# Stages 1 and 2 of a four-stage transformer block in a new order: batch 0 normalised on chip, six matmuls of constants ahead of the first weight

## The chip, the cores and the metric

The kernel runs on one core of a Trainium2 chip. The metric is the device time in microseconds (us) of one execution; lower is better. The five engines run side by side and are kept in step by semaphores: TensorE (PE, weight loads shown as PEld), VectorE (DVE), ScalarE (ACT), GpSimd (POOL) and SyncE (SP), which here only issues DMAs.

## What is computed

Input `x` is 4 batches of 512 tokens and 512 features in float32. Four residual stages follow one another, each on the layer-normalised stream:

```python
x = x + gelu(einsum('bds,st->bdt', ln(x), einsum('ds,td->st', w1, w2) * sparse_mask) + b2)   # stage 1
x = x + ffn(ln(x), ffn_weight, ffn_bias, centroids, assignments)                             # stage 2
x = x + attention(ln(x), Wqkv, bqkv, Wo, bo)                                                 # stage 3
x = x + ffn(ln(x), ffn_weight, ffn_bias, centroids, assignments)                             # stage 4

def ffn(x, weight, bias, centroids, assignments):
    hits = softmax(x @ centroids.T / 0.1) > 0.01
    rows = any(hits, axis=0)[assignments]          # one mask of output rows, over ALL tokens
    return where(any(hits, axis=1)[:, None] & rows[None, :], x @ weight.T + bias, 0)
```

The row mask of stages 2 and 4 needs the cluster hits of all 2048 tokens, so stage 3 can't begin before the last token of stage 2 has its logits.

## The kernel before

**Tiling.** A tile is 128 tokens by 512 features; there are 16, `n = 4 b + t` for batch `b` (`NB` = 4) and tile `t` (`TPB` = 4). `KC` = 4 is the number of 128-wide chunks of a feature axis. A float32 product is made of three fast matmuls on operands split in a rounded high part (`_hi`, written by ScalarE) and the rest (`_lo`, by VectorE or GpSimd): a_hi w_hi + a_lo w_hi + a_hi w_lo. The helper `products` (L991 to L999) issues these, so nearly all matmuls carry line L997; one tile of a 512 x 512 product is 12 matmuls of 128x512. PSUM has four banks for transposes (`t_bank`) and four for products (`m_bank`), used in turn.

**One list of steps.** `schedule()` (L31) writes one list of steps (kind, what, batch, tile). Each engine's program walks the same list and issues what it has in each step, so the list is the order of every engine's queue, and an engine that waits in a step holds all its later steps. The steps that matter here:
- `w2`, `w1` c: ScalarE and VectorE split a chunk of the two stage-1 weights. `M attn` c: TensorE multiplies it, 12 matmuls (L1070 to L1076 for the first chunk, L997 behind).
- `mask_attn` (L857, VectorE): times the sparse mask. `colmean` (L1091, TensorE): column means by a matmul with a constant. `center_attn` (L871, VectorE), `split_attn` (L739 ScalarE, L861 VectorE): subtract the means, split. The centred weight stands in for the mean of the layer norm, so `y1` can be made from raw `x` and scaled by `rstd` afterwards.
- `split_x` (L721 ScalarE, L647 GpSimd): splits `x` transposed, which comes from memory transposed (`xt`). `M y1`: 12 matmuls a tile. `scaled` (L892 VectorE) scales and adds b2, then Gelu (L735 ScalarE); `x1` (L898 VectorE) adds it to the stream.
- `stats` (L845, L846 VectorE; L635, L636 GpSimd, for stage 3 also `nbias` L639): variance and `rstd` = variance to the power -0.5, per tile. `norm` (L694 ScalarE): the normalised tile, for stage 3.
- `center_f`, `center_c` (L882 VectorE, L652 and L656 GpSimd, L725 and L730 ScalarE): centre the stage-2 weight and the centroids. `T` (L1060 TensorE): four transposes to a t_bank; its `hi` is L715 (ScalarE) and its `lo` L832 (VectorE), step `lo`.
- `M cl2` (L1125): cluster logits of a batch, 8 matmuls; `T tc2`, `logit2`, `prob2`: their softmax (L801 ScalarE, L953 to L974 VectorE). `M dn2`: the dense product of a tile; ScalarE evacuates it (L759), GpSimd adds the bias (L663). `best2`, `mask2` (L1164, L1171): the row mask. `early`: a part of a product issued ahead of the rest.

**Order.** In stages 1 and 2 a loop over batches 1 to 3 does, for each tile, `T x2` of the batch before, `M y1`, `lo x2`, the residual with its stats, `scaled`; then `M cl2` of the batch before; then four `M dn2` of it, beside stats and `split_x` of the next batch.

**DMA queue.** SP issues in this order: eight chunks of w2 and w1 (256 KB each), `ffn` (1 MB), `cen`, `sparse` (1 MB), `x` of batch 0 (1 MB), `xt` of batch 0 in two halves (1 MB), b2, `x` of batch 1. Then it waits for the last `T ffn` and issues `xt` 1 and more.

## Time and profile before

| | us |
|---|---|
| three runs | 330.07, 329.35, 327.91 |
| median | 329.35 |
| profiled execution, whole | 328.85 |
| its span, first to last instruction | 327.0 |

All rows come from the one profiled execution; times in them are us from the start of its span unless marked ns. A row of the waits names the engine and line that waited, what released it, and the total, the count and the longest. A row of the stretches gives the busy time of each engine with its count of instructions, then PEclk, TensorE's granted clock as a share of 2.4 GHz, whose low level, 1.2 GHz, is 0.5. Matmuls are pipelined: their busy times overlap, and the distance from start to start is what one costs. Mean granted clock over the span: 0.950.

### The profile page before, as it was taken

To read this page: it belongs to the slowest core of one execution; us is meant where nothing else is said; L and a number is where in the kernel's file an instruction comes from. 1 tells how busy PE (TensorE), PEld (TensorE's weight loads), DVE (VectorE), ACT (ScalarE), POOL (GpSimd) and SP (SyncE) were. 2 spreads that over 40 slices of the span, in tenths; PEclk is the share of its full clock that TensorE was granted. 3 is DMA by queue.
4 is the path that set the end of the run, shared out by engine and by line. 5 is a ranking of instruction groups with operands and counts; after the bars stand their busy time and mean duration, and the time that the engine had idled before them with its cause. 6 is when DMAs were issued, how large, how long until landed. Compare 5 with 4: busy or idle time off the path is not lost.

```text
span 327.0 us, 4206 instructions
## 1 busy us (share of the span) xinstructions
PE 282.6 (86%) x1356; PEld 228.5 (70%) x1356; DVE 243.7 (75%) x450; ACT 146.8 (45%) x266; POOL 166.2 (51%) x246
## 2 busy tenths in 40 slices
PE   3966939899969979977999899999997999988790
PEld 3835828688858868756988687878785787867670
DVE  3697588684777467867279769789787897689796
ACT  5463432275237423637266346752537526514300
POOL 1046059379747913318934379174952665117221
PEclk9995978999979997999899999999999999999976
DMA  7990488300000000000000000000000000000066
GB/s 234 355 357 1 157 293 299 121 3 0 0 2 0 1 0 2 0 0 2 0 1 0 3 0 3 0 0 2 0 1 1 2 0 0 2 0 0 2 256 258
DMA packets 11013, 19.27 MB, mean 59 GB/s; under 512 B 1072, under 2 KB 2608, under 8 KB 10992
## 3 DMA queue, kind: packets, MB, share of 16 engines
q1 hardware_dynamic: 10992, 19.01, 16.8%
q8 instruction: 11, 0.18, 0.2%
q14 instruction: 10, 0.08, 0.1%
HBM read 14.81 MB, written 4.19 MB: 58 GB/s over the span
## 4 chain that ended last, share of the span: by engine, by line
PE 43%; DVE 30%; issue 9%; ACT 8%; POOL 5%; DMA 3%; SPq 1%; DVEq 0%; ACTq 0%
PE m_bank L997 34%; DVE st L845 5%; PE t_bank L1060 4%; PE m_bank L1125 4%; DMA xt_other<-in_L_ffn_weight 3%; DVE x_tok L898 3%; DVE y_tok L892 2%; ACT even_hi L715 2%; DVE even_lo L832 2%; DVE x_tok L912 2%; DVE w2t_lo L832 2%; DVE y_tok L904 2%; DVE x_tok L917 2%; POOL rstd L636 2%; DVE mx L936 2%
## 5 line engine op out<-in xcount | busy, mean ns | idle before, releaser
L635 POOL TENSOR_SCALAR ve<-mv 128x1 f32<-128x1 f32 x64 | 16.6, 259 | 99.5 <-DVE mv L846 99.1
L663 POOL TENSOR_TENSOR y_tok<-y_tok,bias_f 128x512 f32<-128x512 f32 x32 | 42.3, 1335 | 30.0 <-ACT y_tok L759 30.0
L845 DVE BATCH_NORM_STATS2 st<-x_tok 128x6 f32<-128x512 f32 x64 | 44.2, 691 | 1.7
L759 ACT ACTIVATE y_tok<-m_bank,rstd 128x512 f32<-128x512 f32 x32 | 21.9, 684 | 44.5 <-PE m_bank L997 44.4
L636 POOL TENSOR_TENSOR rstd<-ve,half 128x1 f32<-128x1 f32 x64 | 37.1, 580 | 5.3
L997 PE MATMUL m_bank<-ffn_hi,even_hi 128*128 128x512 f32 x96 | 39.2, 409 | 0.0
L997 PE MATMUL m_bank<-ffn_lo,even_hi 128*128 128x512 f32 x96 | 37.6, 392 | 0.0
L997 PE MATMUL m_bank<-ffn_hi,even_lo 128*128 128x512 f32 x96 | 37.5, 390 | 0.0
L997 PE MATMUL m_bank<-attn_hi,odd_hi 128*128 128x512 f32 x64 | 28.3, 442 | 10.1 <-POOL odd_lo L647 10.1
L832 DVE TENSOR_TENSOR even_lo<-t_bank,even_hi 128x512 fp32r<-128x512 f32 x24 | 16.2, 685 | 22.9 <-ACT even_hi L715 22.9
L735 ACT ACTIVATE y_tok<-y_tok 128x512 f32<-128x512 f32 x16 | 10.0, 630 | 42.1 <-DVE y_tok L892 42.1
L997 PE MATMUL m_bank<-attn_lo,odd_hi 128*128 128x512 f32 x64 | 26.5, 415 | 0.0
L997 PE MATMUL m_bank<-attn_hi,odd_lo 128*128 128x512 f32 x64 | 26.5, 413 | 0.0
L997 PE MATMUL m_bank<-odd_hi,wqkv_hi 128*128 128x512 f32 (+1 forms) x60 | 22.5, 375 | 0.7 <-DVE odd_lo L832 0.6
L832 DVE TENSOR_TENSOR odd_lo<-t_bank,odd_hi 128x512 fp32r<-128x512 f32 x24 | 15.8, 681 | 9.6 <-ACT odd_hi L715 9.5
L997 PEld LDWEIGHTS m_bank<-attn_hi,odd_hi 128*128 128x128 f32 x64 | 13.1, 205 | 13.0 <-DVE y_tok L892 5.7
L997 PE MATMUL m_bank<-odd_lo,wqkv_hi 128*128 128x512 f32 (+1 forms) x60 | 21.6, 361 | 0.0
L997 PE MATMUL m_bank<-odd_hi,wqkv_lo 128*128 128x512 f32 (+1 forms) x60 | 21.6, 360 | 0.0
L997 PEld LDWEIGHTS m_bank<-ffn_lo,even_hi 128*128 128x128 f32 x96 | 18.1, 188 | 4.0
L674 POOL TENSOR_TENSOR x_tok<-x_tok,bo 128x512 f32<-128x512 f32 x16 | 20.7, 1298 | 0.0
L997 PEld LDWEIGHTS m_bank<-ffn_hi,even_lo 128*128 128x128 f32 x96 | 18.2, 190 | 3.3
L997 PEld LDWEIGHTS m_bank<-ffn_hi,even_hi 128*128 128x128 f32 x96 | 18.2, 190 | 3.2
(142 smaller groups left out, 717.5 us busy)
## 6 DMA issues: line engine op xcount, KB each, us to landing
x_tok<-in_L_attn_a_x SPq DMA_DIRECT2D x4, 1024.0 KB, 10.9
out<-x_tok SPq DMA_DIRECT2D x16, 256.0 KB, 2.2
xt_other<-in_L_attn_a_xt SPq DMA_DIRECT2D x2, 1024.0 KB, 5.2
w_raw<-in_L_attn_a_w SPq DMA_DIRECT2D x4, 256.0 KB, 4.5
y_tok<-in_L_attn_a_w SPq DMA_DIRECT2D x4, 256.0 KB, 4.9
xt_other<-in_L_ffn_weight SPq DMA_DIRECT2D x1, 1024.0 KB, 8.7
y_tok<-in_L_attn_a_sparse_mask SPq DMA_DIRECT2D x1, 1024.0 KB, 10.4
xn_odd<-in_L_attn_a_xt SPq DMA_DIRECT2D x2, 512.0 KB, 13.4
```

The costliest lines, as they stand in the source:

```text
L635: link(pool.tensor_scalar(ve[:, i:i + 1], mv[:, i, 1:2], EPS, None, ALU.add))
L636: ins = pool.tensor_tensor(rstd[:, i:i + 1], ve[:, i:i + 1], half[:, :], ALU.pow)
L663: pool.tensor_tensor(y_tok[:, n, :], y_tok[:, n, :], bias_f[:, :], ALU.add).then_inc(biased, 1)
L674: pool.tensor_tensor(x_tok[:, n, :], x_tok[:, n, :], bo[:, :], ALU.add).then_inc(bo_added, 1)
L735: act.activation(gelu[:, n % 2, :], gelu[:, n % 2, :], ACT.Gelu).then_inc(gelu_done, 1)
L759: act.activation(y_tok[:, n, :], bank[:, :], ACT.Identity, scale=rstd[:, i:i + 1]).then_inc(m_act, 1)
L832: dve.tensor_tensor(lo, bank_view(what, t_bank[j % T_BANKS]), f32(hi), ALU.subtract).then_inc(t_free, 1)
L845: link(dve.bn_stats(st[:, at % 2, :], x_tok[:, n, :]))
L898: dve.tensor_tensor(x_tok[:, n, :], x_tok[:, n, :], gelu[:, n % 2, :], ALU.add).then_inc(x1_done, 1)
L997: ins = pe.matmul(bank, a, w, start=(first and n == 0), stop=(last and n == count - 1))
L1060: ins = pe.transpose(bank[:, c * r:(c + 1) * r], blk, ident[0:r, 0:r])
L1125: ins = pe.matmul(bank[:, tokens], cen_hl[:, c, :], a[:, c, tokens], start=(c + h == 0), stop=(c == KC - 1 and h == 1))
```

## The change

- Batch 0 of stage 1 is normalised on chip: `stats`, `rstd` and `norm` of its tiles, transposes `T x1` of the normalised tiles and their split take the place of `xt` of batch 0. Its `y1` is multiplied by the uncentred weight (`split_raw`, new), with no scale behind it. The centred weight is made later and used by batches 1 to 3. `split_attn`'s low part moves from VectorE to GpSimd.
- `rstd` becomes a step of its own: one tile at a time for stage 1 batch 0 and for stage 3; otherwise (stage 1 of batches 1 to 3, stages 2 and 4) one instruction for the four tiles of a batch.
- In the loop over batches, `T x2` of a batch moves beside `M dn2` of the one before, `M cl2` goes behind a `y1` or `dn2` tile, and stats of stage 2 move behind `scaled`. In the tail, `cl2` of the last batch is issued in two halves and a third `dn2` tile comes ahead of the mask.
- SP's queue: `x` of batch 0 comes in two halves right behind the weights, then `sparse`, b2, `ffn`, `x` 1; `xt` of batch 0 is gone; `cen` comes behind a wait for the last `T x1`.
- TensorE issues `WARM` = 6 matmuls of constants (identity by a constant matrix, 128 columns each) before its first step.

The diff, cut to its core (lines removed from `schedule()` are left out, the order before is told above):

```diff
@@ -23,6 +23,7 @@
 SCALE = float(DH) ** -0.5
 T_BANKS = 4
 M_BANKS = 4
+WARM = 6
 FREED_BY_VECTOR = ("attn", "y1", "q", "k", "pv", "wo")
@@ -63,94 +64,133 @@
         step(what, "", b, t)
         step("stats", stage, b, t)
+        if stage == 3 or t == TPB - 1:
+            step("rstd", stage, b, t)
     for c in range(KC):
         step("w2", "", 0, c)
         step("w1", "", 0, c)
+        if c == KC - 1:
+            for t in range(TPB):
+                step("stats", 1, 0, t)
+                step("rstd", 1, 0, t)
+                step("norm", 1, 0, t)
+            step("T", "x1", 0, 0)
+            step("T", "x1", 0, 1)
         step("M", "attn", 0, c)
+    step("lo", "x1", 0, 0)
+    step("lo", "x1", 0, 1)
+    step("T", "x1", 0, 2)
+    step("T", "x1", 0, 3)
+    step("mask_attn", "", 0, 0)
+    step("mask_attn", "", 0, 1)
+    step("split_raw", "", 0, 0)
+    step("mask_attn", "", 0, 2)
+    step("split_raw", "", 0, 1)
+    step("mask_attn", "", 0, 3)
+    step("split_raw", "", 0, 2)
+    step("split_raw", "", 0, 3)
+    step("lo", "x1", 0, 2)
+    step("lo", "x1", 0, 3)
+    step("M", "y1", 0, 0)
+    step("M", "y1", 0, 1)
     for c in range(KC):
         step("center_f", "", 0, c)
...
     step("colmean", "", 0, 0)
...
+    step("scaled", "", 0, 0)
+    step("scaled", "", 0, 1)
+    step("M", "y1", 0, 2)
     step("center_attn", "", 0, 0)
     for t in range(1, TPB):
         step("center_attn", "", 0, t)
         step("split_attn", "", 0, t - 1)
     step("split_attn", "", 0, TPB - 1)
...
+    step("x1", "", 0, 0)
+    step("T", "ffn", 0, 0)
+    step("M", "y1", 0, 3)
+    step("scaled", "", 0, 2)
+    step("split_x", "", 1, 0)
+    step("split_x", "", 1, 1)
     step("lo", "ffn", 0, 0)
...
+    step("x1", "", 0, 1)
+    step("T", "ffn", 0, 1)
     step("T", "ffn", 0, 2)
     step("T", "ffn", 0, 3)
...
+    step("scaled", "", 0, 3)
+    step("lo", "ffn", 0, 1)
+    step("x1", "", 0, 2)
     step("lo", "ffn", 0, 2)
...
     step("lo", "ffn", 0, 3)
...
+    step("x1", "", 0, 3)
+    step("split_x", "", 1, 2)
+    step("split_x", "", 1, 3)
+    step("center_c", "", 0, 0)
+    for t in range(TPB):
+        step("stats", 1, 1, t)
+    step("rstd", 1, 1, TPB - 1)
     step("T", "cen", 0, 0)
...
     for b in range(1, NB):
         for t in range(TPB):
...
+            if b == 1:
+                step("T", "x2", 0, t)
             step("M", "y1", b, t)
...
+            if b == 1:
+                if t == 0:
+                    step("lo", "cen", 0, 0)
+                step("lo", "x2", 0, t)
+            if t:
+                step("x1", "", b, t - 1)
+                if b == NB - 1:
+                    step("stats", 2, b, t - 1)
             step("scaled", "", b, t)
...
+            if b == 1:
+                step("stats", 2, 0, t)
+            elif t == 0:
+                step("M", "cl2", b - 1, 0)
+            elif t == 1:
+                step("T", "tc2", b - 1, 0)
+                step("logit2", "", b - 1, 0)
+            elif t == 2:
+                step("prob2", "", b - 1, 0)
+        if b == 1:
+            step("rstd", 2, 0, TPB - 1)
+            step("onehot", "", 0, 0)
+        if b == NB - 1:
+            break
+        for t in range(TPB):
+            step("M", "dn2", b - 1, t)
+            if b == 1 and t == 0:
+                step("M", "cl2", 0, 0)
+            if t == 0:
+                step("x1", "", b, TPB - 1)
+            if b == 1 and t == 1:
+                step("T", "tc2", 0, 0)
+                step("logit2", "", 0, 0)
+            step("T", "x2", b, t)
+            step("lo", "x2", b, t)
+            step("stats", 2, b, t)
+            step("split_x", "", b + 1, t)
+            step("stats", 1, b + 1, t)
+            if b == 1 and t == 2:
+                step("prob2", "", 0, 0)
+        step("rstd", 2, b, TPB - 1)
+        step("rstd", 1, b + 1, TPB - 1)
     b = NB - 1
     step("T", "x2", b, 0)
     step("T", "x2", b, 1)
+    step("x1", "", b, TPB - 1)
     step("lo", "x2", b, 0)
...
     step("lo", "x2", b, 1)
     step("T", "x2", b, 2)
+    step("M", "dn2", b - 1, 0)
+    step("lo", "x2", b, 2)
     step("T", "x2", b, 3)
...
     step("lo", "x2", b, 3)
...
+    step("stats", 2, b, TPB - 1)
+    step("rstd", 2, b, TPB - 1)
     last_batch_clusters(step, 2)
     residual("x2", 3, 0, 0)
     residual("x2", 3, 0, 1)
...
@@ -306,19 +346,26 @@
 def last_batch_clusters(step, stage):
     b, dense = NB - 1, f"dn{stage}"
-    if stage == 4:
-        step("early", "cl4", b, 0)
+    step("early", f"cl{stage}", b, 0)
     step("M", f"cl{stage}", b, 0)
+    if stage == 2:
+        step("M", dense, b - 1, 1)
     step("T", f"tc{stage}", b, 0)
     step(f"logit{stage}", "", b, 0)
     if stage == 4:
         step("blend", 4, b - 1, TPB - 1)
+    else:
+        for t in range(TPB):
+            step("blend", 2, 0, t)
     step("M", dense, b, 0)
     step("M", dense, b, 1)
+    if stage == 2:
+        step("M", dense, b, 2)
     step(f"prob{stage}", "", b, 0)
     step(f"best{stage}", "", 0, 0)
     step(f"mask{stage}", "", 0, 0)
-    step("M", dense, b, 2)
+    if stage == 4:
+        step("M", dense, b, 2)
 def program(nc, x_d, xt_d, w1_d, w2t_d, b2_d, sparse_d, wqkv_d, bqkv_d, wo_d, bo_d, ffn_d, fb_d, cen_d,
...
@@ -551,32 +607,29 @@
                 rows_c = slice(c * P, (c + 1) * P)
                 sp.dma_start(w2_raw[:, c, :], w2t_d[rows_c, :]).then_inc(ld_w2[c], 16)
                 sp.dma_start(w1_raw[:, c, :], w1_d[rows_c, :]).then_inc(ld_w1[c], 16)
+            for h in range(2):
+                sp.dma_start(x_tok[:, 2 * h:2 * h + 2, :], rows_of(x_d[0][2 * h * P:(2 * h + 2) * P, :])).then_inc(ld_x0[h], 16)
+            sp.dma_start(sparse, rows_of(sparse_d)).then_inc(ld["sparse"], 16)
+            sp.dma_start(b2[:, :], b2_d.rearrange("(a n) -> a n", a=1).broadcast_to([P, D])).then_inc(ld["b2"], 16)
             sp.dma_start(ffn_raw[:, :, :], rows_of(ffn_d)).then_inc(ld["ffn"], 16)
+            load_x(1)
+            sp.wait_ge(t_done, T_AT["x1", 0, TPB - 1] + 1)
+            load_xt(1)
             sp.dma_start(cen_raw, cen_d).then_inc(ld["cen"], 16)
-            sp.dma_start(sparse, rows_of(sparse_d)).then_inc(ld["sparse"], 16)
-            load_x(0)
-            early, late = slice(0, S // 2), slice(S // 2, S)
-            sp.dma_start(xt_raw[0][:, :, early], rows_of(xt_d[0][:, early])).then_inc(ld["xt0"], 16)
-            sp.dma_start(xt_raw[0][:, :, late], rows_of(xt_d[0][:, late])).then_inc(ld["xt0_late"], 16)
-            sp.dma_start(b2[:, :], b2_d.rearrange("(a n) -> a n", a=1).broadcast_to([P, D])).then_inc(ld["b2"], 16)
-            load_x(1)
-            sp.wait_ge(t_done, T_AT["ffn", 0, KC - 1] + 1)
-            load_xt(1)
             sp.dma_start(bias_f[:, :], fb_d.rearrange("(a n) -> a n", a=1).broadcast_to([P, D])).then_inc(ld["bias_f"], 16)
+            load_x(2)
             sp.dma_start(bqkv[:, :], bqkv_d.rearrange("(j p) -> p j", p=P),
                           allow_slow_non_contiguous=True).then_inc(ld["small"], 16)
             sp.dma_start(assign, assign_d.rearrange("(a n) -> a n", a=1).broadcast_to([P, D])).then_inc(ld["small"], 16)
-            load_x(2)
+            sp.wait_ge(t_done, T_AT["ffn", 0, KC - 1] + 1)
+            load_xt(2)
             load_x(3)
-            sp.wait_ge(x_split, TPB)
-            load_xt(2)
             sp.wait_ge(attn_split, KC)
             sp.dma_start(wo_raw, wo_d).then_inc(ld["wo"], 16)
             sp.dma_start(wqkv_raw, rows_of(wqkv_d)).then_inc(ld["wqkv"], 16)
             sp.dma_start(bo[:, :], bo_d.rearrange("(a n) -> a n", a=1).broadcast_to([P, D])).then_inc(ld["bias"], 16)
-            sp.wait_ge(x_split, 2 * TPB)
+            sp.wait_ge(x_split, TPB)
             load_xt(3)
             outs = [b * TPB + t for kind, _, b, t in STEPS if kind == "out"]
             for at, n in enumerate(outs):
...
@@ -627,25 +680,34 @@
             for kind, what, b, t in STEPS:
                 n = b * TPB + t
-                if kind == "stats":
-                    at = STAT_AT[what, b, t]
-                    i = (what - 1) * NT + n
-                    pool.wait_ge(stats_done, at + 1)
-                    link(pool.tensor_scalar(ve[:, i:i + 1], mv[:, i, 1:2], EPS, None, ALU.add))
-                    ins = pool.tensor_tensor(rstd[:, i:i + 1], ve[:, i:i + 1], half[:, :], ALU.pow)
-                    if what == 3:
+                if kind == "rstd":
+                    single = (what, b, 0) in RSTD_AT
+                    i = (what - 1) * NT + (n if single else b * TPB)
+                    k = 1 if single else TPB
+                    pool.wait_ge(stats_done, STAT_AT[what, b, t] + 1)
+                    link(pool.tensor_scalar(ve[:, i:i + k], mv[:, i:i + k, 1], EPS, None, ALU.add))
+                    ins = pool.tensor_tensor(rstd[:, i:i + k], ve[:, i:i + k], half[:, 0:k], ALU.pow)
+                    if single:
                         link(ins)
                         ins = pool.tensor_scalar(nbias[:, i:i + 1], mv[:, i, 0:1], rstd[:, i:i + 1], -1.0, ALU.mult,
                                                  ALU.mult)
                     ins.then_inc(rstd_done, 1)
-                    if (what == 2 and b >= 1 or what == 1 and b >= 2) and pieces:
-                        split_late(*pieces.pop(0))
+                elif kind == "stats":
+                    if what == 1 and b >= 2 or what == 2 and b == NB - 1:
+                        for _ in range(2 if what == 1 else 1):
+                            if pieces:
+                                split_late(*pieces.pop(0))
                 elif kind == "split_x":
-                    pool.wait_ge(x_hi_done, n + 1)
+                    pool.wait_ge(x_hi_done, n - TPB + 1)
                     pool.tensor_tensor(feat(odd_lo, t), feat(xt_raw[b % 2], t), f32(feat(odd_hi, t)),
                                        ALU.subtract).then_inc(x_split, 1)
+                elif kind == "split_attn":
+                    pool.wait_ge(attn_hi_done, t + 1)
+                    pool.tensor_tensor(attn_lo[:, t, :], attn_f[:, t, :], f32(attn_hi[:, t, :]),
+                                       ALU.subtract).then_inc(attn_split, 1)
                 elif kind == "center_f":
...
@@ -732,7 +794,13 @@
                 elif kind == "scaled":
                     act.wait_ge(*m_freed(M_AT["y1", b, t]))
-                    act.activation(gelu[:, n % 2, :], gelu[:, n % 2, :], ACT.Gelu).then_inc(gelu_done, 1)
+                    act.activation(gelu_of(n), gelu_of(n), ACT.Gelu).then_inc(gelu_done, 1)
+                elif kind == "split_raw":
+                    act.wait_ge(*m_freed(M_AT["attn", 0, t]))
+                    if t == KC - 1:
+                        act.wait_ge(m_done, M_AT["attn", 0, KC - 1] + 1)
+                    act.activation(raw_hi[:, t, :], attn_f[:, t, :], ACT.Copy).then_inc(raw_hi_done, 1)
                 elif kind == "split_attn":
...
@@ -884,18 +957,25 @@
                 elif kind == "scaled":
                     dve.wait_ge(m_done, M_AT["y1", b, t] + 1)
+                    bank = m_bank[M_AT["y1", b, t] % M_BANKS][:, :]
                     if n == 0:
                         dve.wait_ge(ld["b2"], 16)
-                    dve.wait_ge(rstd_done, STAT_AT[1, b, t] + 1)
-                    if n >= 2:
+                    if n == TPB:
+                        dve.wait_ge(attn_split, KC)
+                    if n % TPB >= 2 or n >= TPB + 2:
                         dve.wait_ge(x1_done, n - 1)
-                    dve.scalar_tensor_tensor(out=gelu[:, n % 2, :], in0=m_bank[M_AT["y1", b, t] % M_BANKS][:, :],
-                                             scalar=rstd[:, n:n + 1], in1=b2[:, :], op0=ALU.mult,
-                                             op1=ALU.add).then_inc(m_dve, 1)
+                    if b == 0:
+                        dve.tensor_tensor(gelu_of(n), bank, b2[:, :], ALU.add).then_inc(m_dve, 1)
+                    else:
+                        rstd_ready(dve, 1, b, t)
...
@@ -988,6 +1068,9 @@
         def _(pe):
             pe.wait_ge(consts, 6)
+            for _ in range(WARM):
+                pe.matmul(m_bank[M_BANKS - 1][:, 0:P], ident[:, :], mean_of[:, :], start=True, stop=True)
             def products(bank, pairs, first=True, last=True):
...
                     ins.then_inc(t_done, 1)
                 elif kind == "M" and what == "y1" and n == 0:
                     pair = [(m_free_for(M_AT["y1", 0, i]), slice(i * P, (i + 1) * P)) for i in range(2)]
-                    pe.wait_ge(x_split, 2)
+                    split_ready("x1", 0, 1)
                     for c in range(KC):
-                        pe.wait_ge(attn_split, c + 1)
+                        pe.wait_ge(raw_split, c + 1)
                         for tile_bank, cols in pair:
                             ins = products(tile_bank, [((odd_hi[:, c, cols], odd_lo[:, c, cols]),
-                                                        (attn_hi[:, c, :], attn_lo[:, c, :]))],
+                                                        (raw_hi[:, c, :], raw_lo[:, c, :]))],
                                            first=c == 0, last=c == KC - 1)
                             if c == KC - 1:
                                 ins.then_inc(m_done, 1)
@@ -1112,8 +1195,14 @@
```

## Rows read from the trace of the kernel before

**Rows 1.** Page, part 1: busy time and share of each engine.
```profile
PE 282.6 (86%) x1356; PEld 228.5 (70%) x1356; DVE 243.7 (75%) x450; ACT 146.8 (45%) x266; POOL 166.2 (51%) x246
```
**Rows 2.** Waits over the whole span (total us, times, longest), TensorE's two largest.
```profile
PE m_bank L997 <- POOL odd_lo L647: 10.1, 2, 5.5
...
PE m_bank L1125 <- DVE even_lo L832: 6.0, 3, 2.5
```
**Rows 3.** Busy time by stretches (engines' busy us and counts, PEclk, DMA share, GB/s).
```profile
47.90:62.50 14.60, 14.54 (x60) 11.54 (x60) 11.40 (x22) 4.94 (x10) 10.64 (x19) 0.85 0.75 267
...
92.70:120.60 27.90, 27.84 (x124) 22.53 (x124) 19.27 (x35) 12.78 (x22) 16.61 (x24) 0.94 0.00 1
```
**Rows 4.** Chain that ended last, three pieces: start us, us, what.
```profile
4.48 8.72 DMA xt_other<-in_L_ffn_weight
...
27.19 7.84 PE m_bank L997 x24
...
66.06 2.73 PE m_bank L997 x12
```
**Rows 5.** Timeline of TensorE: start us, us, line, op, out<-in, [idle before <-releaser].
```profile
4.94 2.05 PE L1070 MATMUL m_bank<-w2t_hi,even_hi 128*128 128x512 f32 x4 [4.94 <-ACT even_hi L685]
...
17.95 3.70 PE L1091 MATMUL t_bank<-y_tok,mean_of 128*128 128x512 f32 x8 [0.55 <-DVE y_tok L857]
...
47.89 0.76 PE L997 MATMUL m_bank<-attn_hi,odd_hi 128*128 128x512 f32 x1 [5.48 <-POOL odd_lo L647]
...
53.05 0.48 PE L997 MATMUL m_bank<-attn_hi,odd_hi 128*128 128x512 f32 x1
...
56.24 0.48 PE L997 MATMUL m_bank<-attn_hi,odd_hi 128*128 128x512 f32 x1
...
120.20 0.39 PE L997 MATMUL m_bank<-attn_lo,odd_hi 128*128 128x512 f32 x1
...
122.47 0.47 PE L1125 MATMUL m_bank<-even_hi,cen_hl 128*128 128x512 f32 x1 [1.89 <-DVE even_lo L832]
...
144.76 0.47 PE L1171 MATMUL m_bank<-onehot,csel 128*128 128x512 f32 x1 [0.68 <-DVE csel L984]
```
**Rows 6.** Groups by line and form: xcount | busy us, mean ns | idle before, releasers.
```profile
L845 DVE BATCH_NORM_STATS2 st<-x_tok 128x6 f32<-128x512 f32 x64 | 44.2, 691 | 1.7
...
L636 POOL TENSOR_TENSOR rstd<-ve,half 128x1 f32<-128x1 f32 x64 | 37.1, 580 | 5.3
...
L635 POOL TENSOR_SCALAR ve<-mv 128x1 f32<-128x1 f32 x64 | 16.6, 259 | 99.5 <-DVE mv L846 99.1
...
L832 DVE TENSOR_TENSOR even_lo<-t_bank,even_hi 128x512 fp32r<-128x512 f32 x24 | 16.2, 685 | 22.9 <-ACT even_hi L715 22.9
...
L715 ACT ACTIVATE even_hi<-t_bank 128x512 fp32r<-128x512 f32 x24 | 13.7, 586 | 0.0
...
L694 ACT ACTIVATE xn_odd<-x_tok,nbias,rstd 128x512 f32<-128x512 f32 x16 | 13.0, 813 | 8.1 <-POOL nbias L639 8.1
...
L846 DVE BATCH_NORM_AGGREGATE mv<-st 128x2 f32<-128x6 f32 x64 | 11.7, 182 | 2.2
...
L647 POOL TENSOR_TENSOR odd_lo<-xn_odd,odd_hi 128x512 fp32r<-128x512 f32 x8 | 10.9, 1374 | 2.4 <-ACT odd_hi L721 2.4
...
L639 POOL TENSOR_SCALAR nbias<-mv,rstd 128x1 f32<-128x1 f32 x16 | 4.8, 299 | 1.7
...
L861 DVE TENSOR_TENSOR attn_lo<-y_tok,attn_hi 128x512 fp32r<-128x512 f32 x4 | 4.1, 1037 | 0.2
...
L735 ACT ACT_TABLE_LOAD x3 | 3.8, 1283 | 0.1
...
L850 DVE TENSOR_TENSOR even_lo<-y_tok,even_hi 128x512 fp32r<-128x512 f32 x4 | 2.8, 692 | 0.4 <-ACT even_hi L685 0.4
...
L730 ACT ACTIVATE lg<-lg,fmean 64x512 f32<-64x512 f32 x1 | 0.7, 722 | 0.0
```
**Rows 7.** Timeline of ScalarE, the split of the last w2 chunk.
```profile
9.32 0.63 ACT L682 ACTIVATE w2t_hi<-w_raw 128x512 fp32r<-128x512 f32 x1 [0.49 <-DMA w_raw<-in_L_attn_a_w]
```

127 lines of the change are left out of this document (46 added, 81 removed).

## The prediction

> **What bounds the kernel now.** I read the header of the page first, then the waits, the busy time by stretches, the chain, and last TensorE's timeline around its gaps. The header shows TensorE busy for 282.6 of 327.0 us, the next engine (VectorE) for 243.7 [rows 1]. So the kernel is held by TensorE, and what an edit can win is the time in which TensorE stands still or runs at its low clock. The waits say where: 10.1 us on GpSimd's `odd_lo` (twice) and 6.0 us on VectorE's `even_lo` (three times, ahead of the `cl2` logits) [rows 2]. All of these lie before 123 us, in stages 1 and 2; the change ends there too, apart from one matmul group that moves ahead of the mask.
>
> Each gap costs twice. After the 5.48 us gap ahead of the first `y1` tile of batch 1 (47.89) the stretch 47.9 to 62.5 has a mean granted clock of 0.85 [rows 3, 5]. Low is half of full, so 0.30 of 14.6 us, 4.4 us, ran at 1.2 GHz and cost 2.2 us. By the same reckoning 92.7 to 120.6 (0.94) lost 1.7 us [rows 3]. The first `y1` pair shows it directly: 24 matmuls took 7.84 us, where 12 at full clock take 2.73 [rows 4].
>
> **The sum, from TensorE's side.** From 47.89 to 120.6 (the last `y1` matmul starts at 120.20, 0.4 us long) 72.7 us pass [rows 5]. The work in it is 12 `y1` tiles and 8 `dn2` tiles of 2.73 us (54.6), 12 `x2` transposes at 0.47 (a tile and its transpose take 3.19, 53.05 to 56.24 [rows 5]; 5.6), two `cl2` of 8 matmuls (3.8) and two `tc2` (0.7): 64.7 us. The other 8.0 are the waits ahead of `cl2` (6.0 less the 1.89 of the third, so 4.1) and 3.9 of low clock. That closes the account, so I can price the new order by the same items.
>
> **Part 1: the head, up to the first `y1` tile of batch 1.** Batch 0 is now normalised from `x`, so `xt` of batch 0 (1 MB) is not loaded, and `x` of batch 0 stands right behind the weights in SP's queue, where `ffn` stood. The last `w2` chunk was in at 9.32 [rows 7]; behind it came 0.25 MB of `w1` and 1 MB of `ffn`, in by 13.2 [rows 4], 0.32 MB per us. Half of `x` is then in at about 11.7, the rest at 13.2. A tile needs stats on VectorE (0.69 and 0.18), `ve`, `rstd` and `nbias` on GpSimd (0.26, 0.58, 0.30 and the steps between, 1.25) and `norm` on ScalarE (0.81) [rows 6]. GpSimd passes a tile each 1.25 us, so tiles 0 and 1 are normalised at 14.7 and 16.0. TensorE has their transposes in front of the last `attn` chunk, so that chunk ends near 19.3. Behind it VectorE has in a row two `lo`, four masks, four `split_raw` and two `lo`, twelve operations of 0.61 to 0.69 [rows 6]: 19.2 to 27.0. The `y1` pair can start at 22.5 instead of 27.2 because it multiplies the uncentred weights and no longer waits for `colmean`. It ends at 28 to 29.6 by clock, `colmean` (3.5 us, as its row has it [rows 5]) at 32, `y1` 2 and 3 at 38 and the `ffn` transposes at 39. Before, TensorE was through the same at 42.4 (47.89 less 5.48 [rows 5]). That is 3.4 us won, and nearly all of it is lost in the next wait. `split_attn` moves to GpSimd, and begins there only when `colmean`, the centring and, on ScalarE, the Gelu table load (1.28) and two Gelus are over, at about 34.3. Four of them and four `split_x` follow at 1.3 to 1.45 us each [rows 6]: GpSimd is done at 45.3. `center_c` stands behind them in its queue, then 0.72 on ScalarE [rows 6], and TensorE has `T cen` in front of batch 1. Everything behind `T cen` on TensorE waits too. The first tile of batch 1 starts at 47.4: 0.5 us won, again from a cold clock (gap of some 7 us).
>
> **Part 2: the interleaving of batches 1 to 3.** In batch 1, `stats 2` now comes after `scaled`, out of the loop of VectorE, Gelu, `hi` and `lo`; this shortens the loop by 0.87 us a tile (0.69 and 0.18 [rows 6]). `dn2` of the batch before goes ahead of `cl2` (b=1) or `y1` of the next batch does (b=2, 3), so each `cl2` has a tile of 2.73 us to cover the `hi` and `lo` (0.59 and 0.69 [rows 6]) that it waits for. Both waits, 4.1 us, go, and the low clock that followed them, 1.7 us. The stretch now also holds the third `cl2` and `tc2` (2.3). It takes 64.7 + 2.3 + 2.2 of cold start = 69.2 us and ends at 116.6, against 120.6. I checked the others: in the second half of b=1 VectorE has about 14.3 us of work (eight stats 7.0, four `lo` 2.7, the rest logits, probabilities and one `x1`) beside 15.1 of TensorE's, with no room ahead of `cl2` 1; GpSimd 16 us. The grouped `rstd` (one of 4 columns for four of one) takes 21 pairs of 0.26 and 0.58 off GpSimd [rows 6], which is what lets it carry the late splits; no row shows a 4-column `pow`. I bound it between 0.58 and four times that, take 0.8, and even at 2.3 it lies beside `y1` tiles, whose banks give it some 8 us. Stage 4 loses twelve such pairs as well; GpSimd waited 99.5 us ahead of `ve` [rows 6], so they had nothing behind them, and I price that at 0.
>
> **Part 3: the tail of stage 2.** Work behind the last `y1`: `dn2` 2,0 and 2,1 and three of batch 3 (13.7), transposes (1.8), `cl2` in two halves (2.0), best and mask (1.4), and waits for `x1` of tile 14 and the split of tile 15, 1.2 us: 20.1 us. Mask at 136.7 instead of 144.76 [rows 5]: 8.1 us earlier. One `dn2` tile of the two behind the mask is already done; there the chain of stats, GpSimd and `norm` sets the pace, so I take 0.7 for it (0 to 1.5). From there everything is unchanged. Sum: 8.8 us.
>
> **Part 4: six matmuls of constants.** The constants are written by 2.1 us, the first weight is split at 4.94 [rows 5]. Nearest row: `colmean`, eight passes of 512 columns at 0.44 [rows 5]; a quarter of the columns and twelve passes give 1.3 us at full and 2.6 at low clock, so they fit. They are hidden: nothing waits for them. What can they win? The first four matmuls took 2.05 us against 0.91 for four at full clock [rows 4, 5], 1.1 us. But TensorE then stands before `T x1` until 14.8 either way, so I price it at 0 (bounds: 1.1 won, 0.3 lost if they run late). The Trainium skill, "TensorE: Matmul & The Clock Gate", part 1, says the throttled state is the default and activity releases it; by that rule the first weights would run at full clock. The slow first four agree.
>
> **What speaks against moving `split_attn`.** The same subtraction with two inputs in SBUF took VectorE 0.69 in the first stage (L850, GpSimd idle) and 1.04 as L861 beside GpSimd's `odd_lo`, itself 1.37 [rows 6]. From 34 to 45 us, and in the b=1 loop, GpSimd is now busy all the time. I add 0.8 us for what slips because of it (0 to 3). The Trainium skill, "GPSIMD Engine Reference", section 1, says that GpSimd shares its SBUF interfaces with VectorE and collides with instructions of two SBUF inputs; these rows agree.
>
> So 8.8 less 0.8: 8.0 us. The span goes from 327.0 to 319.0. The profiled execution took 328.85, 1.85 around its span, so 320.85; I say 320.8. It lies 0.5 below the median of the runs, 329.35.
>
> **Rivals.**
> Forecast, 318.3 to 323: chance 0.55.
> A, contention: GpSimd holds `center_c` longer (eight operations at 1.6 to 1.8 us: 2 to 3 us) and VectorE slips ahead of `cl2` 1 by 1 to 2. Gain 3 to 6, time about 324. For it: VectorE has no slack at that `cl2`. Against: the three other engines have slack elsewhere. 0.17.
> B, more: the first pair finds a full clock, the six matmuls help by 1.1, the tail's waits vanish. Gain 10.5 to 13, time about 317. 0.17.
> B also holds the clock rule as a mechanism alone: 1.1 us more, 319.7, if `x` landed before 10 us and TensorE did not wait for it; 0.05 of the forecast's chance.
> C, no effect to be seen: the low clock also takes the last `attn` chunk (2.7 us) and another wait ahead of a `cl2` returns (4 us). 326 to 332, about 328: 0.07.
> D, slower: the path from `x` landing to the first tile of batch 1 has no slack, so each us that `x` is late is one us of the end. It decides from 8.0 + 3.3 = 11.3 us of delay: `x` in at 23 instead of 11.7. Before, `x` stood behind `ffn`, `cen` and `sparse`, 2.1 MB, at 0.32 MB per us 6.6 us more; even that would leave a gain of 1.4. Time if it comes at 23.5 us: 333. 0.04.
>
> **Numbers.** About 1% (3.3 us) is what a measurement can tell: faster means below 326. The forecast, A and B are faster: 0.86 after the part of A that falls short. Same 0.10, slower 0.04. The range 316.5 to 325.5 leaves out the lower end of B, and C and D.
>
> **What would show it.** Right: `T x1` 0 at about 14.8 and the `y1` pair at about 22.5; a gap of about 7 us ended by ScalarE's `lg` (`center_c`) with batch 1's first tile at 47.4; no wait ahead of `cl2` 0, 1 and 2; last `y1` at 116.6; mask at 136.7; the clock full from 52 us to the tail. Wrong: a first tile later than 50 us, a `cl2` gap over 1 us, or operations of two SBUF inputs over 1.2 us throughout. If the mask moves by 8 us and the time by less, the front of stage 3 took it.

## The result, and the profile after

| kernel | median of its runs, us | profiled span, us | mask2, us | span behind mask2, us |
|---|---|---|---|---|
| before | 328.63 (4 runs, beside the next) | 327.0 | 144.76 | 182.24 |
| changed | 332.14 (331.38 to 332.75, 4 runs) | 330.3 | 145.69 | 184.61 |
| changed, again | 332.43 (7 runs; before 329.16) | 330.1 | 147.34 | 182.76 |

Medians are over all runs of a kernel; two runs of those below lie over 1.5% above the fastest of their kernel (322.64 with three edits and `WARM` 0, 332.02 with the bias additions moved), and the ratios leave them out.

The change made the kernel slower by 1%: ratio 1.0103 (95% interval 1.0053 to 1.0153), and 1.0127 (1.0089 to 1.0166) in the second comparison. I had said 320.8. The span is 330.3 where my sum gave 319.0: 11.3 us to explain.

First the header of the page of the changed kernel, and TensorE's timeline at the places that I had named (columns as in [rows 5]; L1143 are transposes, L1080 products, L1214 `cl2`, L1260 the mask).

```profile
PE 287.9 (87%) x1392; PEld 234.6 (71%) x1392; DVE 238.8 (72%) x454; ACT 154.7 (47%) x276; POOL 147.6 (45%) x184
```
```profile
2.19 2.93 PE L1072 MATMUL m_bank<-mean_of,ident 128*128 128x128 f32 x12 [2.19 <-POOL cluster L659]
4.91 1.87 PE L1153 MATMUL m_bank<-w2t_hi,even_hi 128*128 128x512 f32 x4
6.62 1.08 PE L1156 MATMUL m_bank<-w2t_lo,even_hi 128*128 128x512 f32 x4
...
13.89 0.60 PE L1143 MATMUL t_bank<-ident,xn_odd 128*128 128x128 f32 x4
...
21.57 0.47 PE L1080 MATMUL m_bank<-even_hi,odd_hi 128*128 128x512 f32 x1 [2.24 <-DVE even_lo L934]
...
46.02 0.66 PE L1143 MATMUL t_bank<-ident,lg 64*128 64x64 f32 x4 [8.06 <-ACT lg L792]
...
47.38 0.78 PE L1080 MATMUL m_bank<-attn_hi,odd_hi 128*128 128x512 f32 x1
...
80.57 0.47 PE L1214 MATMUL m_bank<-even_hi,cen_hl 128*128 128x512 f32 x1 [1.22 <-DVE even_lo L903]
...
89.81 1.09 PE L1143 MATMUL t_bank<-ident,lg 128*128 128x128 f32 x4 [4.43 <-ACT lg L838]
...
124.49 0.40 PE L1080 MATMUL m_bank<-attn_lo,odd_hi 128*128 128x512 f32 x1
...
145.69 0.47 PE L1260 MATMUL m_bank<-onehot,csel 128*128 128x512 f32 x1 [0.67 <-ACT y_tok L830]
```

The head came out as forecast: first tile of batch 1 at 47.38 (47.4 said). The last `y1` tile starts its last matmul at 124.49 and ends with `T x2` at 124.72, where 116.6 was said. So 8.1 of the 11.3 us are lost between 47.4 and 124.7, and there stands a wait of 4.43 us, at `T tc2` 1, that my text does not have. The other 3.2 are in the tail (145.69 less 124.7 is 21.0, 20.1 said) and behind the mask (184.61, where I had 182.24 less 0.7 and plus the 0.8 for contention, 182.3).

Whose wait is it? The same stretch on GpSimd, VectorE and ScalarE (L704 low part of x^T, L679 late pieces of wqkv, L689 and L690 `ve` and `rstd`, L973 `scaled`, L797 Gelu, L838 `lg`):

```profile
81.77 1.28 POOL L704 TENSOR_TENSOR odd_lo<-xt_other,odd_hi 128x512 fp32r<-128x512 f32 x1
83.02 1.98 POOL L679 TENSOR_TENSOR wqkv_lo<-y_tok,wqkv_hi 128x384 fp32r<-128x384 f32 x2
84.97 0.22 POOL L689 TENSOR_SCALAR ve<-mv 128x4 f32<-128x4 f32 x1
85.27 1.04 POOL L690 TENSOR_TENSOR rstd<-ve,half 128x4 f32<-128x4 f32 x1
86.29 0.23 POOL L689 TENSOR_SCALAR ve<-mv 128x4 f32<-128x4 f32 x1
86.60 1.02 POOL L690 TENSOR_TENSOR rstd<-ve,half 128x4 f32<-128x4 f32 x1
```
```profile
87.77 0.75 DVE L973 SCALAR_TENSOR_TENSOR y_tok<-m_bank,rstd,rows 128x512 f32<-128x512 f32 x1 [5.73 <-POOL rstd L690]
```
```profile
88.56 0.63 ACT L797 ACTIVATE y_tok<-y_tok 128x512 f32<-128x512 f32 x1 [9.36 <-DVE y_tok L973]
89.09 0.58 ACT L838 ACTIVATE lg<-m_bank 128x512 f32<-128x512 f32 x1
```

Read it backwards. `T tc2` 1 waits for `lg`; `lg` needs only `cl2` 1, whose matmuls are through at about 82.5, but in ScalarE's queue it stands behind Gelu 2,0 (the Gelu of batch 2, tile 0); Gelu waits for `scaled` 2,0, which waits for `rstd` of stage 1, batch 2. The last statistics of that batch were ready at 82.04, and GpSimd then had a low part, two late pieces and the four columns of *stage 2* ahead of it. So `rstd` was there at 87.62, 5.6 us behind its statistics, and only 1.3 of these are its own two operations.

The busy time by stretches shows the second price (last columns: granted clock, DMA share, GB/s):

```profile
47.40:63.90 16.50, 16.50 (x73) 13.53 (x72) 11.98 (x24) 4.58 (x8) 1.83 (x4) 0.90 0.31 95
63.90:80.60 16.70, 15.48 (x79) 12.57 (x77) 10.80 (x26) 11.25 (x19) 10.00 (x12) 1.00 0.00 0
80.60:89.80 9.20, 4.78 (x20) 3.63 (x21) 2.71 (x6) 1.11 (x2) 8.10 (x9) 0.92 0.00 0
89.80:101.00 11.20, 11.19 (x41) 9.17 (x42) 6.87 (x15) 5.89 (x9) 0.00 (x0) 0.76 0.01 1
101.00:124.70 23.70, 23.40 (x113) 19.13 (x112) 15.98 (x35) 12.02 (x21) 14.77 (x14) 1.00 0.00 1
```

Behind the wait TensorE is busy without a pause and granted only 0.76 of the clock, which costs 0.24 of 11.2 us, 2.7 us. [rows 3] had 0.94 for the 27.9 us from 92.7, 1.7 us lost.

### The profile page after: what moved, and what is told of

Read it like the earlier page. It is cut to its first block, busy times and chain, and to the rows that moved or that the text cites. A ratio compares the mean times of both kernels' runs of the same rounds, so it can differ in the third digit from the quotient of the medians.

```text
span 330.3 us, 4237 instructions
## 1 busy us (share of the span) xinstructions
PE 287.9 (87%) x1392; PEld 234.6 (71%) x1392; DVE 238.8 (72%) x454; ACT 154.7 (47%) x276; POOL 147.6 (45%) x184
## 4 chain that ended last, share of the span: by engine, by line
PE 38%; DVE 22%; POOL 17%; ACT 9%; issue 9%; DMA 2%; SPq 1%; DVEq 0%; ACTq 0%; POOLq 0%
PE m_bank L1080 31%; POOL odd_lo L704 5%; PE t_bank L1143 4%; POOL rstd L690 3%; DVE st L918 3%; PE m_bank L1214 2%; POOL y_tok L725 2%; DVE x_tok L992 2%; DVE w2t_lo L903 2%; DMA x_tok<-in_L_attn_a_x 2%; POOL attn_lo L709 2%; DVE x_tok L997 2%; DVE odd_lo L903 2%; DVE mx L1016 2%; DVE y_tok L973 2%
## 5 line engine op out<-in xcount | busy, mean ns | idle before, releaser
L689 POOL TENSOR_SCALAR ve<-mv 128x1 f32<-128x1 f32 (+1 forms) x31 | 8.8, 283 | 113.6 <-DVE mv L919 113.1
L1080 PE MATMUL m_bank<-ffn_hi,even_hi 128*128 128x512 f32 x96 | 39.3, 409 | 0.0
L1080 PE MATMUL m_bank<-ffn_lo,even_hi 128*128 128x512 f32 x96 | 37.7, 393 | 0.0
L1080 PE MATMUL m_bank<-ffn_hi,even_lo 128*128 128x512 f32 x96 | 37.4, 390 | 0.0
L903 DVE TENSOR_TENSOR odd_lo<-t_bank,odd_hi 128x512 fp32r<-128x512 f32 x28 | 18.3, 682 | 14.6 <-ACT odd_hi L778 14.3
L797 ACT ACTIVATE y_tok<-y_tok 128x512 f32<-128x512 f32 x16 | 10.0, 631 | 34.6 <-DVE y_tok L973 33.9
L690 POOL TENSOR_TENSOR rstd<-ve,half 128x1 f32<-128x1 f32 (+1 forms) x31 | 23.5, 757 | 2.6
L756 ACT ACTIVATE xn_odd<-x_tok,nbias,rstd 128x512 f32<-128x512 f32 x20 | 16.3, 814 | 16.9 <-POOL nbias L693 16.9
L1080 PE MATMUL m_bank<-odd_hi,wqkv_hi 128*128 128x512 f32 (+1 forms) x60 | 22.9, 381 | 0.2
L1080 PE MATMUL m_bank<-odd_lo,wqkv_hi 128*128 128x512 f32 (+1 forms) x60 | 22.0, 366 | 0.0
L1080 PE MATMUL m_bank<-odd_hi,wqkv_lo 128*128 128x512 f32 (+1 forms) x60 | 21.9, 365 | 0.0
L1080 PE MATMUL m_bank<-attn_hi,odd_hi 128*128 128x512 f32 x48 | 21.3, 443 | 0.0
L1080 PEld LDWEIGHTS m_bank<-ffn_lo,even_hi 128*128 128x128 f32 x96 | 18.0, 188 | 4.0
L1080 PEld LDWEIGHTS m_bank<-ffn_hi,even_lo 128*128 128x128 f32 x96 | 18.1, 189 | 3.1
L1080 PEld LDWEIGHTS m_bank<-ffn_hi,even_hi 128*128 128x128 f32 x96 | 18.1, 188 | 3.1
L1080 PE MATMUL m_bank<-attn_hi,odd_lo 128*128 128x512 f32 x48 | 20.1, 420 | 0.0
L1080 PE MATMUL m_bank<-attn_lo,odd_hi 128*128 128x512 f32 x48 | 20.0, 416 | 0.0
```

The source lines that it names most:

```text
L689: link(pool.tensor_scalar(ve[:, i:i + k], mv[:, i:i + k, 1], EPS, None, ALU.add))
L690: ins = pool.tensor_tensor(rstd[:, i:i + k], ve[:, i:i + k], half[:, 0:k], ALU.pow)
L756: act.activation(xn_odd[:, t, :], x_tok[:, n, :], ACT.Identity, bias=nbias[:, i:i + 1], scale=rstd[:, i:i + 1]).then_inc(norm_done, 1)
L797: act.activation(gelu_of(n), gelu_of(n), ACT.Gelu).then_inc(gelu_done, 1)
L903: dve.tensor_tensor(lo, bank_view(what, t_bank[j % T_BANKS]), f32(hi), ALU.subtract).then_inc(t_free, 1)
L1080: ins = pe.matmul(bank, a, w, start=(first and n == 0), stop=(last and n == count - 1))
```

## The experiments

Each is the changed kernel with the edit named. Gains below are against 332.14 unless another kernel is named; in every comparison the kernel before ran on the same chip (327.9 to 329.2), and ratios are to it. A wait or a time inside a kernel is read from one profiled execution of it.

**1. Is it the order on ScalarE, or `rstd`?** Three remedies for one wait.

```diff
+            if b > 1 and t == 0:
+                step("M", "cl2", b - 1, 0)      # its lg now stands ahead of the Gelu
             step("scaled", "", b, t)
-            elif t == 0:
-                step("M", "cl2", b - 1, 0)
```


> Only the place of ScalarE's copy of cl2 1 and cl2 2 into lg changes: it stands ahead of the Gelu of the same batch, not behind it. Theory: T tc2 1 no longer waits 4.43 us at 85.4, the low clock that follows (0.76 from 89.8 to 101) goes too, and the time falls by 4 to 6 us to 326 to 328. Rival 1 (rstd is late for scaled itself, so y1 banks stop TensorE next): the wait moves to y1 2,3 or T x2 2,0, and no more than 1.5 us is won, 330.5 or above. Rival 2 (VectorE is the bound of the body of batches 1 to 3): no change, 332 within 0.7.

Measured: 328.57, ratio 0.9997 (0.9966 to 1.0028): 3.6 us won, a little less than the 4 to 6 expected. The wait at `T tc2` 1 is gone and the last `y1` matmul comes at 117.42, 7.1 us earlier, but `mask2` only 1.7 earlier (143.96). The time comes back as a wait of TensorE for batch 3's `x1`, and the cause is again GpSimd:

```profile
123.79 1.09 PE L1143 MATMUL t_bank<-ident,x_tok 128*128 128x128 f32 x4 [3.67 <-DVE x_tok L978]
```
```profile
113.74 0.75 DVE L973 SCALAR_TENSOR_TENSOR y_tok<-m_bank,rstd,rows 128x512 f32<-128x512 f32 x1 [5.44 <-POOL rstd L690]
```

So the edit hid one late `rstd`, and the next, of batch 3, stood behind it: its last statistics were there at 108.29, its result at 113.61.

```diff
-        step("rstd", 2, b, TPB - 1)
         step("rstd", 1, b + 1, TPB - 1)
+        step("rstd", 2, b, TPB - 1)
```
and GpSimd's last two late pieces of the b=1 loop are popped behind both.

> On GpSimd the rstd of stage 1, batch b+1 stands ahead of that of stage 2, batch b, and the last two late pieces of wqkv/wo behind both. Theory: rstd of stage 1 batch 2 is there at about 84.4 instead of 87.7, Gelu 2,0 ends near 85.8, lg at 86.4 and T tc2 1 waits about 1 us instead of 4.43: 3 to 4.5 us won, 327.6 to 329.1. Rival 2 (VectorE or TensorE's clock is the bound there, the wait only shows it): less than 1 us won, 331.2 or above. Rival 3 (work pushed back on GpSimd makes dn2 1,0's bias or the late pieces late): a new wait behind 90, and no gain.

Measured: 325.91, ratio 0.9899 (0.9855 to 0.9943): 6.2 us won, more than the 3 to 4.5 expected. The `rstd` of stage 1 now stands right behind the low part, the wait at `T tc2` 1 is 1.19, and `mask2` is at 142.21:

```profile
84.03 1.29 POOL L707 TENSOR_TENSOR odd_lo<-xt_other,odd_hi 128x512 fp32r<-128x512 f32 x1
85.29 0.23 POOL L689 TENSOR_SCALAR ve<-mv 128x4 f32<-128x4 f32 x1
85.59 1.04 POOL L690 TENSOR_TENSOR rstd<-ve,half 128x4 f32<-128x4 f32 x1
```
```profile
88.82 0.63 PE L1146 MATMUL t_bank<-ident,lg 128*128 128x128 f32 x4 [1.19 <-ACT lg L841]
```

The whole edit is an order on GpSimd, an engine that is busy 45% of the time.

```diff
             step("stats", 1, b + 1, t)
+            step("rstd", 1, b + 1, t)           # per tile
-        step("rstd", 1, b + 1, TPB - 1)
```


> The changed kernel with one part undone: the rstd of stage 1, batches 2 and 3, is made for each tile right behind its statistics, as in the kernel before, not for all four at the end. Theory (the grouped rstd at the end of GpSimd's queue is what makes T tc2 1 wait): the first tile's rstd is there 10 us before it is needed, both the 4.43 at 89.8 and the wait of batch 3's x1 go, mask2 comes at 140 to 142 and the time is 326 to 328, in spite of some 2.7 us more of GpSimd's time for each batch. Rival (GpSimd is simply too full in batch 1's loop, in whatever order): its longer queue makes the split of batch 2's x^T late, a wait of 2 us or more stands at y1 2,2 or 2,3, and the time is 331 or above.

Measured: 330.27, ratio 1.0026 (0.9989 to 1.0062): 1.9 us won where 4 to 6 were expected. The 4.43 is gone and the last `y1` comes 3.6 us earlier (120.86), but `mask2` is at 145.05. Both theories had a part: the grouped `rstd` does make the first wait, and the per-tile one takes more of GpSimd's time, also since it makes an `nbias` (0.26) for each tile that the kernel before did not make here. The last `rstd` of batch 3 and that of stage 2 come at 116 to 118.7, and TensorE waits 2.48 for `x1` at 124.6; the wait of 2 us at `y1` 2,2 or 2,3 that the rival named isn't there.

**2. The late `T cen`.**

```diff
     for c in range(KC):
         step("center_f", "", 0, c)
+    step("center_c", "", 0, 0)
...
-    step("center_c", "", 0, 0)                  # stood behind split_x 1,3
```


> center_c stands right behind center_f on VectorE, GpSimd and ScalarE, ahead of the four low parts of x^T of batch 1; T cen keeps its place. Theory: T cen 0 follows T ffn 3 at 38 instead of 46.0, and y1 1,0 waits only for GpSimd's first low parts, to about 40.7; from there VectorE's x1 and stats of batch 1 (to 47.6) and the rstd behind them set the pace, so of the 6.7 us gained at the tile only 2.5 to 4 are left at the end: 328.1 to 329.6. Rival 2 (VectorE sets the pace of the body from its first tile): all of it is given back, 331.5 to 332.5. Rival 4 (the load of the centroids lands late and holds VectorE's queue): slower than 332.5.

Measured: 322.57, ratio 0.9812 (0.9773 to 0.9851): 9.6 us won, where I had expected 2.5 to 4 from a gap of 8.06. The first tile of batch 1 starts at 41.87, 5.5 earlier, with a full clock (47.4 to 63.9 had 0.90):

```profile
41.87 0.47 PE L1080 MATMUL m_bank<-attn_hi,odd_hi 128*128 128x512 f32 x1 [0.41 <-POOL odd_lo L704]
```
```profile
42.00:54.00 12.00, 12.00 (x59) 9.93 (x60) 10.37 (x23) 3.45 (x7) 5.77 (x5) 1.00 1.01 342
```

`mask2` is at 140.57, 5.1 earlier; the other 4.5 us of the span lie behind it (180.13 against 184.61), where no instruction differs. Against the second profile of the changed kernel it is 6.8 and 2.6. More on that under 5.

**3. Is it the head or the loops?** The lines of the diff from the loops on are put back; what had to be added for the new head:

```diff
             step("M", "y1", b, t)
+            if b == 1:
+                step("stats", 2, 0, t)
+                if t == TPB - 1:
+                    step("rstd", 2, 0, t)
             step("lo", "x2", b - 1, t)
```


> The new head (batch 0 normalised on chip, warm-up, T cen late) with the loops, the tail and the mask's neighbours in the order of the kernel before, stats 2 of batch 0 in the first loop. Theory: the head brings batch 1's first tile at 47.4 against 47.9 and nothing is lost or won by it; with the old loops (96.9 from there to mask2) mask2 comes at about 144 and the time is 327 to 329, so the new loops are what costs 3 to 5 us beside the changed kernel's 332.1. Rival (the head's own work, by contention or by the clock, makes what follows slow): 331 or above.

Measured: 329.26, ratio 1.0026 (0.9993 to 1.0059). As far as these runs can tell, the new head costs nothing and wins nothing; the waits ahead of `cl2` are back (1.38, 3.79 and 1.50, against 6.0 in all in [rows 2]) and `T tc2` 1 has none. The loss of the changed kernel is in its loops and its tail, which this edit puts back together.

**4. All together, and further.**

The diffs of `center_c`, of `lg` and of `rstd` in one kernel:

> The three edits together: center_c right behind center_f, lg of cl2 ahead of the Gelu, stage 1's rstd ahead of stage 2's and of the last late pieces. Theory (late T cen and late lg are two separate waits, the second with two remedies that overlap): mask2 at 136 to 137 where center_c alone had 140.57 (its wait of 2.78 at T tc2 1, and the low clock on both sides of it, go), and the time is 317 to 320. Rival (VectorE sets the pace once TensorE starts batch 1 at 41: cl2 1 waited 2.90 for the low part of x2 with center_c alone): mask2 at 139 to 140, 321 to 322.5. If the three gains simply added up: 332.1 - 9.6 - 6.2 - 3.6 = 312.7; I expect that not to be so, since two of them cure the same wait.

Measured: 319.47, ratio 0.9746 (0.9699 to 0.9793), `mask2` at 135.66. As expected, not the sum.

```diff
-    if stage == 2:
-        step("M", dense, b, 2)
     step(f"prob{stage}", "", b, 0)
     step(f"best{stage}", "", 0, 0)
     step(f"mask{stage}", "", 0, 0)
-    if stage == 4:
-        step("M", dense, b, 2)
+    step("M", dense, b, 2)
```


> The three edits together, and stage 2's dn2 3,2 behind mask2 as in the kernel before. Theory: mask2 comes about 2.7 us earlier than without this edit, but TensorE has one product more behind it and stage 3's first transposes wait for VectorE's mask chain all the same: the span behind mask2 grows by 1.5 to 2.7, and the time is within 1 us of the three edits' own, a little better (0.5) if the work then fills the wait that T x3 has at 150. Rival (the order at the mask is the cause of the loss behind it, 184.6 in the changed kernel against 182.2): 2 us or more less than the three edits.

Measured: 319.32, ratio 0.9736 (0.9668 to 0.9803). `mask2` came 1.6 earlier and the stretch behind it was 1.1 shorter in the profiled executions, yet the medians are the same: undecided, and no cause of the loss.

The wait of 2.91 at `cl2` 1 that these kernels show at 76 was taken next: `logit2` of batch 0 behind the low part of `x2` 1,1, and each `prob2` a tile later.

```diff
+            step("T", "x2", b, t)
             if b == 1 and t == 1:
                 step("T", "tc2", 0, 0)
-                step("logit2", "", 0, 0)
-            step("T", "x2", b, t)
             step("lo", "x2", b, t)
+            if b == 1 and t == 1:
+                step("logit2", "", 0, 0)
...
-            if b == 1 and t == 2:
+            if b == 1 and t == 3:
                 step("prob2", "", 0, 0)
```


> The three edits and dn2 3,2 behind mask2 (319.3 before), and now the softmax of batch 0's clusters out of the way: T tc2 0 behind T x2 1,1, its logit step behind the low part of x2 1,1, and all prob2 steps one tile later. Theory (cl2 1 waits 2.91 at 76 since the four exps, 2.7 with their table, stand ahead of the high parts on ScalarE and prob2, 2.0, ahead of the last low part on VectorE): the wait falls to under 1, and the time to 316.5 to 318. Rival (the pace there is set by dn2's evacuations and the rstd of stage 2, which ScalarE waits for at 61.5): the wait stays above 2, and the time at 319 within 1.

Measured: 318.28, ratio 0.9687 (0.9626 to 0.9748). The wait is gone and the last `y1` comes at 109.56 instead of 112.58, but `mask2` at 134.70 instead of 134.04: `rstd` of batch 3 is through at 104.28, 3.6 us behind its statistics, and TensorE waits 3.60 at `T x2` 3,2.

```diff
     step("T", "x2", b, 1)
+    step("M", "dn2", b - 1, 0)
     step("x1", "", b, TPB - 1)
...
     step("T", "x2", b, 2)
-    step("M", "dn2", b - 1, 0)
```


> The same, and dn2 2,0 ahead of T x2 3,2 instead of behind it: it fills the 2.27 us that TensorE waited for x1 3,2. Theory: mask2 comes 1 to 2 us earlier than without it, and the time is 315 to 317. Rival (VectorE's x1, Gelu and low parts of batch 3 end the stage, whatever TensorE does meanwhile): mask2 as without it within 0.5, since cl2 3 then waits for the low parts.

Measured: 320.65, ratio 0.972 (0.9651 to 0.9789), `mask2` at 137.06. The theory fell: the wait only moved to `T x2` 3,3 (3.25). The rival had the mechanism, a tail paced by `x1` 3, but not the size: `mask2` came 2.4 later than without the edit, where it allowed 0.5. 1.0 of this was there at the first `y1` of batch 1 already, and the intervals of the two kernels overlap, so whether the edit costs time is undecided.

Then the cause was taken away: the additions of `bias_f` to `dn2` of the batch before, 1.3 us each, put behind both `rstd` on GpSimd, on two bases: the kernel of 318.28 with the softmax of batch 0's clusters moved, and the kernel with `rstd` first.

```diff
+    for b in range(1, NB - 1):
+        first, last = o.index(("M", "dn2", b - 1, 0)), o.index(("rstd", 2, b, TPB - 1))
+        late = [s for s in o[first:last] if s[0] == "bias_f"]
+        kept = [s for s in o[first:last + 1] if s[0] != "bias_f"]
+        o[first:last + 1] = kept + late
     return o
```


> All edits but the one of the tail: center_c early, lg ahead of Gelu, softmax of batch 0's clusters later, dn2 3,2 behind mask2, rstd first and bias_f behind it. Without the last it took 318.3, with mask2 at 134.7 and a wait of 3.60 for x1 3,2 at 115.3, which is rstd of batch 3 at 104.3 behind 13 us of GpSimd's queue. Theory: that rstd comes at about 100, the wait at 115 falls under 1.5, mask2 comes at 131 to 132.5 and the time is 315 to 316.5. Rival (the chain of VectorE and ScalarE over x1 3, low parts and cl2 3 needs its time in any case): mask2 at 134 or later, 318 within 0.8.

Measured: 315.74 (314.64 to 317.09, 6 runs), ratio 0.9616 (0.9587 to 0.9645), `mask2` at 131.81. `rstd` of batch 3 is there at 102.0 instead of 104.3, the wait 1.59 where under 1.5 was expected. This is the fastest kernel of the study, 3.8% faster than the one before.

> The changed kernel with GpSimd's order alone altered: rstd of stage 1 ahead of that of stage 2 and of the last late pieces (325.9 by itself), and the additions of bias_f to dn2 of the batch before (four of 1.3 in each loop) behind both rstd. Theory (the queue ahead of rstd is the cause, in batch 2's loop as in batch 1's): rstd of batch 3 comes 4 to 5 us earlier in its loop, x1 3 no longer holds T x2 3, mask2 comes 2 to 3.5 us earlier than 142.2, and the time is 322.5 to 324.5. Rival (behind the first wait TensorE and its clock set the pace, GpSimd's queue of batch 3 lies beside them): 325.9 within 0.8.

Measured: 329.12 (327.07 to 332.02, 10 runs), ratio 1.0002 (0.9971 to 1.0033): 3.2 us *slower* than without the additions moved. This expectation fell, and with it the idea that each us taken from GpSimd's queue is a us of the end. The `rstd` of batch 3 didn't come 4 to 5 us earlier. In both kernels GpSimd is already waiting for the last statistics when it starts it, so its queue no longer held it; first the kernel with `rstd` first alone, then this one:

```profile
110.89 0.23 POOL L689 TENSOR_SCALAR ve<-mv 128x4 f32<-128x4 f32 x1 [0.40 <-DVE mv L922]
```
```profile
110.75 0.23 POOL L694 TENSOR_SCALAR ve<-mv 128x4 f32<-128x4 f32 x1 [0.54 <-DVE mv L927]
```

Where the time went, by one profile of each. GpSimd's low part now ran beside VectorE's `prob2` of batch 0, whose operations grew (`qsel` 1.11 instead of 0.46, the product 0.89 instead of 0.50); `cl2` 1, behind them, waited 2.26 instead of 1.24, and the clock was low behind it. The stretch 78 to 90, first of this kernel and then of the one with `rstd` first alone:

```profile
78.00:90.00 12.00, 9.74 (x38) 7.64 (x37) 8.81 (x16) 3.49 (x6) 8.96 (x11) 0.86 0.01 2
```
```profile
78.00:90.00 12.00, 9.58 (x46) 7.41 (x45) 8.56 (x18) 4.09 (x6) 11.75 (x13) 1.00 0.01 1
```

From the first `y1` matmul of batch 1 to the last this made only 0.9 us (72.43 against 71.53), and batch 1 had begun 1.0 earlier. The tail, from there to `mask2`, took 1.9 more (23.63 against 21.70): `x1` 3,2 made TensorE wait 1.93 instead of 1.52, and the stretch 120.4 to 126 had 0.79 of the clock instead of 1.00. Another 1.3 lie behind the mask (184.10 against 182.79). So much of the loss is low clock behind waits of about 2 us. That the moved additions bring it is argued, not shown: the ten runs show the loss, not its cause. In the fastest kernel `prob2` stood elsewhere.

**5. The constants, and the clock.**

```diff
-WARM = 6
+WARM = 0
```


> WARM is 0 instead of 6, all else as in the changed kernel. Theory (the loss lies in the late rstd of stage 1, batch 2): the first tile pair of attn_a's product is 4.9 to 6.8 in either case and T x1 0 waits for norm, so the time stays at 332.1 within 0.5. Rival (the six products of constants cost time, or shift the granted clock of the whole): 1 us or more less than the changed kernel, near 331 or below. A third reading, that they hide a slow start: 1.1 us more, 333.2.

Measured: 330.33, ratio 1.0066 (1.0035 to 1.0096). The time is the one that the rival named.

> The three edits together with WARM 0. Theory (the six products of constants hide nothing and cost nothing; the 1.8 us that WARM 0 gave on the changed kernel came from a low clock at 250 to 258 that happened to fall away): within 1 us of the three edits with WARM 6. Rival (the six products cost time by themselves): again 1.5 to 2 us less.

Measured: 320.03, ratio 0.972 (0.9643 to 0.9798), against 319.47 with the six. So on one base 1.8 us less, with intervals that overlap, on the other nothing. In the first no wait from `T cen` to the mask is shorter by more than 0.03; the span behind it is 180.09 instead of 184.61.

> The changed kernel itself once more, for a second profile and a time on the chip of these runs. If the low clock at 250 to 258 belongs to this kernel, it is there again, the span behind mask2 is 184 to 185 and the time 331 to 333. If it fell there by chance of that one execution, the span behind mask2 is 180 to 182.5 as in six variants with the same code behind mask2, and the time may be anything from 329.5 to 332.5. Up to mask2 (145.7 in the first profile) both expect the same within 1.5.

Measured: 332.43; `mask2` 147.34, then 182.76. Both forecasts of the last part missed a little, and `mask2` is 1.6 from the first profile. So 330.3 and 330.1 are one time made of different parts, and part of the 184.61 was that execution's own. Behind the mask the twelve profiled executions of kernels that do not differ there took 180.1 to 184.6. The granted clock goes with it, between 252 and 258 for instance 0.52 in the first profile of the changed kernel, 0.72 in the second and 1.00 in those with `WARM` 0 and with `lg` first, behind a gap of TensorE of 1.75 in all four. (In the two profiles of the changed kernel another gap, of 1.1 to 1.2, stands 2.4 ahead of it. That isn't what decides: the kernel with `rstd` first has only the 1.75 and low clock behind it, the one with both fillings below has both gaps and full clock.) It also orders the runs of one kernel: with `WARM` 0 the three at a mean clock of 0.961 took 329.3 to 329.5, the two at 0.944 took 332.6 and 333.0.

The last two runs take the clock apart from the waits. They leave each wait as it is and let TensorE work through it on products of constants, into the bank that the transposes then fill.

```diff
+FILL = {("cen", 0): 29, ("tc2", 1): 17}         # the first run: tc2 alone
                     bank = t_free_for(j)
+                    for _ in range(FILL.get((what, b), 0)):
+                        pe.matmul(bank[:, 0:P], ident[:, :], mean_of[:, :], start=True, stop=True)
```


> The changed kernel, with 17 products of constants (34 passes, about 4.1 us at full clock) on TensorE ahead of T tc2 1: the wait for lg stays, but TensorE works through it. They go to the bank that the transposes then fill. Theory (wait and clock are two prices of the late rstd, and the second is about 2.5 us: granted clock 0.50 from 89.8 to 95): T tc2 1 still starts at 89.8, y1 2,2 and 2,3 behind it run at full clock, last y1 comes 2 to 3 us earlier and the time is 329.3 to 330.3. Rival (the clock there is slack: batch 3's rstd on GpSimd stops TensorE anyhow): last y1 earlier, mask2 not, 332 within 0.7.

Measured: 330.36, ratio 1.0024 (0.9997 to 1.0052), 1.8 to 2.1 us won. From the first `y1` matmul of batch 1 to the last it took 75.06 us instead of 77.11. The products, `T tc2` 1 behind them (1.1 later here than in the changed kernel, since the head ended 0.7 later), and the stretch from 89.8 to 101:

```profile
86.41 3.96 PE L1119 MATMUL t_bank<-mean_of,ident 128*128 128x128 f32 x34
90.92 0.66 PE L1146 MATMUL t_bank<-ident,lg 128*128 128x128 f32 x4 [0.55 <-ACT lg L839]
```
```profile
89.80:101.00 11.20, 10.65 (x55) 8.78 (x54) 7.45 (x15) 8.14 (x14) 0.27 (x1) 1.00 0.00 0
```

> The same, and 29 such products (58 passes, about 7.1 us) ahead of T cen too, in the wait of 8.06 us there. Theory: batch 1's first two tiles, with 0.54 to 0.77 of the clock granted from 42 to 54, run at full clock, which is worth 1.5 to 3 us more: 326.8 to 328.8. Rival (VectorE, busy to 47.6 and then waiting for rstd of batch 1, sets the pace of the first tiles): 0.5 us or less more than the filling at T tc2 alone.

Measured: 325.70, ratio 0.9929 (0.9893 to 0.9965): 6.4 us less than the changed kernel, and more than I had expected. The time from the end of the work ahead of `T cen` to `T cen` is 7.1 us (8.06 and 7.16 in the two profiles of the changed kernel), that at `T tc2` 1 4.3 (4.43 and 4.46), the wait at `cl2` 1 1.24 (1.22 in both): the waits are those of the second profile to 0.1 us, only filled. Granted clock 1.00 in both stretches:

```profile
47.40:63.90 16.50, 16.50 (x80) 13.64 (x80) 12.65 (x25) 5.05 (x9) 3.00 (x4) 1.00 0.36 125
89.80:101.00 11.20, 11.20 (x55) 9.28 (x54) 7.43 (x17) 7.61 (x13) 2.33 (x3) 1.00 0.01 1
```

The changed kernel had 0.90 and 0.76 in these stretches. From the first matmul of batch 1 to the last of `y1` it took 72.95 us (47.27 to 120.22) against 77.11: the clock's share of batches 1 to 3 is 4.2 us, or 5.0 against the second profile (48.18 to 126.12, 77.94).

## Why the prediction was wrong

**Part 1, the head: right.** `T x1` 0 at 13.9 (14.8), the `y1` pair at 21.6 (22.5), `T cen` in a gap of 8.06 ended by ScalarE's `lg`, batch 1 at 47.38 (47.4). Its weakness is one of judgement: I saw the gap and took it as given, and with `center_c` moved the medians differ by 9.6 us.

**Part 2: the step that failed.** Two sentences of it. The first prices the grouped `rstd` at 0.8 and says that even at 2.3 it "lies beside `y1` tiles, whose banks give it some 8 us". It took 1.04 and 0.22; that was not the error. I asked only how long the operation is and which bank runs out, not what stands ahead of it in GpSimd's queue, and behind which other work its user stands. With the queue it came at 87.62, and its effect reached TensorE not through a bank but through ScalarE's order, Gelu ahead of `lg`. The two edits of one thing each show it: with `rstd` ahead in GpSimd's queue the wait of 4.43 fell to 1.19, with `lg` ahead of the Gelu it was gone. In the latter kernel the stretch up to the last `y1` took 70.5 us (47.18 to 117.65), close to the 69.2 of my sum, though `rstd` was as late as before: so the late `rstd` of batch 2 did lie beside the banks, as I had said; what it did not lie beside was ScalarE's queue. The second is "I checked the others", a total of 16 us for GpSimd beside 15.1 for TensorE: a total shows no lateness, and one above TensorE's should have stopped me. The account of the stretch from 47.4 to 124.7:

| term | said | measured |
|---|---|---|
| work | 67.0 | 67.3 (72.95 of the run with both fillings, less the 5.65 of waits) |
| waits (`cl2` 1, `T tc2` 1) | 0 | 5.65 |
| low clock | 2.2 | 4.2 (77.11 less 72.95; 5.0 by the second profile) |
| sum | 69.2 | 77.1 to 77.3 |

The check is in the first row, where the clock's and the waits' parts are taken off and the work is left as I had it, to 0.3 us. Of the 8.1 us missing, 5.7 are two waits without a term and 2.0 low clock beyond the 2.2 allowed. By the stretches 1.7 were lost behind the gap at `T cen` (0.10 of 16.5), where I had 2.2, and 2.7 behind the wait at `T tc2` 1, where I had nothing.

**Part 3: right to 0.9 us up to the mask, wrong behind it.** 21.0 where I had 20.1. The term held in other kernels too: from the start of the last `y1` matmul to the mask it was 21.2 in the changed kernel, and 21.2 to 21.7 with `center_c` early, with `rstd` first and with the three edits, where the last `y1` came up to 10.6 us earlier. It grew where batch 3's `rstd` was the next thing late: to 26.5 with `lg` first, to 24.2 with `rstd` per tile, and to 25.1 and 26.5 in the two kernels with the softmax moved but not the additions, which even have one `dn2` tile less in it. So my "mask at 136.7" would not have come from curing the wait on ScalarE's side alone (143.96). The 0.7 us for one `dn2` fewer behind the mask are not to be seen: 180.1 to 184.6 there, 182.24 before. The spread by the clock is six times the term.

**Part 4: right in price.** The constants win or cost nothing that two pairs of runs agree on. They do bring the full clock earlier, but not from the first weight on, and how early varies between executions. The first eight matmuls of `attn` took 2.62 us in the first profile of the changed kernel; over all fifteen profiled executions with the constants it was 1.99 to 3.54, the median 2.66, and in the three without them 3.23, 3.46 and 3.55. The second four, in the second profile of the changed kernel and with `WARM` 0, beside 1.08 in the first profile above:

```profile
6.71 1.86 PE L1156 MATMUL m_bank<-w2t_lo,even_hi 128*128 128x512 f32 x4
```
```profile
6.62 1.78 PE L1156 MATMUL m_bank<-w2t_lo,even_hi 128*128 128x512 f32 x4
```

What is won there is slack, since TensorE then waits for `norm`. My bound of 1.1 us was also too high: it compared a duration (2.05) with a distance from start to start (0.91); by the distance (4.94 to 6.79) it is 0.9. The Trainium skill, "TensorE: Matmul & The Clock Gate", part 1, says that activity releases the throttle; my reading of it, that the first weights would run at full clock, did not come true in any of the fifteen (the shortest first four took 1.25 us, at full clock four take 1.08). The rule itself agrees with the earlier rise and with both fillings, where activity held the clock at 1.00.

**Contention** was seen, and small where I put it: VectorE's `x1` took 1.6 to 1.8 beside GpSimd from 33 to 44, 0.69 alone, and still VectorE's part of `center_c` was through at 44.52, before GpSimd came to its own at 44.92. It may have mattered where I did not look, in the run with bias additions moved. "GPSIMD Engine Reference", section 1, of the Trainium skill has the collision for two SBUF inputs; `x1` agrees. `qsel`, with one input, also grew (0.46 to 1.11); the same line names instructions in a 2-port mode, and whether this was one no trace here shows.

**The rivals.** A had the wait at `cl2` 1 (1 to 2 us; 1.22 measured), not the large one. C reached up to 332, but by a low clock in the last `attn` chunk and a returning `cl2` wait of 4 us, and neither was there: that chunk ran at full clock, a matmul each 0.23 us. D, the only slow one, had `x` landing late, and `x` was early. No rival had lateness by an engine's queue order in it, so no mechanism that I named led to 332. A kernel of the time that I forecast does exist, with `center_c`, `lg` and `rstd` moved (319.47), but partly by other means: it starts batch 1 at 41.56, where I had 47.4.

## What to carry to other kernels

When operations are grouped or moved in an in-order queue, follow each of their users, not only its length: write down when its last input is ready, add all that stands ahead of it, then look at what stands behind its first user, on every engine down to TensorE. A wait cured on the user's side (here `lg` ahead of the Gelu) can hide a late producer whose next batch is late too; cure the producer as well, and expect the sum of single gains not to hold. But look first whether the producer waits for its queue or already for its input: in the latter case a shorter queue wins nothing. Price each TensorE gap twice, once for itself and once for the low clock behind it (here 4.43 and 2.7 us), and don't trust a term below 2 us in a stretch where the same code takes 180.1 to 184.6.

## What was unexpected of the hardware

- TensorE kept busy with products of constants through two gaps (34 and 58 passes of 128 columns, 3.96 us for the 34, 6.64 for the 58) gave 6.4 us of 332 back, with the waits as in the second profile of the changed kernel. Six such products ahead of the first weight gave nothing sure.
- The same gap does not always lower the clock. At `cl2` 1 the kernel with three edits waited 2.91 and had 0.72 of the clock behind it, and the same code with `dn2` 3,2 behind the mask waited 2.92 and had 1.00; between 252 and 258 the gap of 1.75 had 0.52, 0.72 or 1.00 behind it in different executions. What decides no run here shows.

```profile
76.00:82.00 6.00, 6.00 (x19) 4.79 (x20) 2.75 (x6) 2.51 (x3) 5.83 (x7) 0.72 0.00 0
```
```profile
76.00:82.00 6.00, 5.74 (x27) 4.81 (x28) 2.77 (x7) 2.52 (x3) 5.83 (x8) 1.00 0.01 3
```

- Small VectorE operations grew beside GpSimd's low parts: 0.69 to 1.6 and 1.8 for two SBUF inputs, 0.46 to 1.11 for a comparison of 4 columns with one input (0.17 in a later batch, where GpSimd was idle).
- GpSimd's `pow` over 4 columns takes 1.02 to 1.33 us, over one 0.57 to 0.58 [rows 6]: grouping four saves about half, not three quarters.
